# Three solve groups, GpSimd's share of the triangular solve, and scaling per group, in a ViT tower kernel

## What is computed

```python
k = x / norm(x); v = (x @ W_write.T) * beta; k_beta = k * beta        # beta = sigmoid(x @ W_beta.T)
A0 = tril(-(k_beta @ k.T * L), -1)                                    # L = decay ** (i - j)
A = solve_triangular(eye - A0, eye, lower=True, unit_diagonal=True)   # 37x37, one per image and head
v_new = A @ v
o = tril(k @ k.T * L) @ v_new
out = x + o @ W_read.T
```

## Time and profile before

| what | value |
|---|---|
| median of three runs | 836.0 us (835.88 to 836.0) |
| the profiled execution | 836.92 us, span of its instructions 835.1 us |
| mean granted TensorE clock | 0.886 of full speed |
| busy share of the span | TensorE 81%, VectorE 54%, ScalarE 27%, GpSimd 31% |

### The profile page before, as it was taken

The page is one execution under the profiler, slowest core; times in us unless marked ns, Lnnn a source line. Parts: engine busy times, 40 slices in busy tenths (PEclk is TensorE's granted clock), DMA queues, the critical chain, the costliest instruction groups (busy, mean ns, idle before and its releaser), DMA issues. The chain is left out here.

```text
span 835.1 us, 13690 instructions
## 1 busy us (share of the span) xinstructions
PE 678.3 (81%) x4562; PEld 519.5 (62%) x4562; DVE 448.1 (54%) x1266; ACT 229.1 (27%) x635; POOL 260.3 (31%) x418
## 2 busy tenths in 40 slices
PE   5899999999977149999983385196569999999994
PEld 4567677777755139999972364085436767667673
DVE  1567777777765742444799199466613333333321
ACT  0223333333322043443431022032013232232321
...
DMA packets 24643, 49.77 MB, mean 60 GB/s; under 512 B 15284, under 2 KB 15414, under 8 KB 23936
## 3 DMA queue, kind: packets, MB, share of 16 engines
...
q10 hardware_dynamic: 288, 4.25, 1.3%
...
## 5 line engine op out<-in xcount | busy, mean ns | idle before, releaser
L1762 PE MATMUL psum<-arena_w,work 128*128 x208 | 95.9, 605 | 1.0 <-DVE work L1814 1.0
L1860 ACT ACTIVATE work<-psum,cst 128x128 f32<-128x128 f32 x208 | 56.6, 383 | 144.1 <-PE psum L1775 144.1
L1786 PE MATMUL psum<-arena_w,work 128*128 x416 | 94.2, 379 | 0.4 <-ACT work L1860 0.4
L1786 PEld LDWEIGHTS psum<-arena_w,work 128*128 128x128 f32 x416 | 77.1, 190 | 10.5 <-issue 1.1
L1724 POOL DMA_INDIRECT out<-work,row_i x26 | 25.8, 990 | 160.2 <-DVE work L1836 160.2
L1823 DVE COPY work<-psum 128x512 f32<-128x512 f32 x52 | 36.0, 692 | 70.0 <-PE psum L1762 61.9
L346 PE MATMUL psum<-arena_w 128*111 128x256 f32 x264 | 64.1, 396 | 4.9 <-DMA arena_w<-in_pack 4.9
L1762 PEld LDWEIGHTS psum<-arena_w,work 128*128 128x128 f32 x208 | 38.3, 194 | 40.1 <-issue 40.1
L711 POOL TENSOR_TENSOR arena_w<-arena_w,work 101x592 f32<-101x592 f32 x33 | 39.6, 1200 | 72.2 <-DVE work L577 72.2
L346 PEld LDWEIGHTS psum<-arena_w 128*111 128x111 f32 x264 | 46.5, 183 | 19.7 <-issue 9.6
L1130 PE MATMUL psum<-tokens,work 111*111 111x128 f32 x88 | 18.2, 340 | 43.4 <-POOL work L1537 43.4
...
...
## 6 DMA issues: line engine op xcount, KB each, us to landing
arena_w<-in_w SPq DMA_DIRECT2D x2, 4096.0 KB, 13.3
...
work<-a_rows SPq DMA_DIRECT2D x21, 32.4 KB, 2.0
```

The lines of the kernel that those rows point to most:

```text
L1762: mm = nc.tensor.matmul(bank[2 * j + f][:, :], xgt[j][:, k * 128:(k + 1) * 128], arena_w1[:, bass.ds(expert * (2 * FF) + (k * FF + f * 512 ...
L1786: mm = nc.tensor.matmul(bank[7][:, 0:D], ht[j][:, g * 128:(g + 1) * 128], arena_w2[:, bass.ds(expert * (FC * D) + g * D, D)], start=(g == ...
L1860: nc.scalar.activation(ht[j][:, g * 128:(g + 1) * 128], bank[4 + f][:, k * 128:(k + 1) * 128], ACT.Gelu, bias=cst[:, bass.ds(expert * FC + ...
```

## The change

There are three groups, pairs 0 to 4, 5 to 7 and 8 to 10; the third has four sets of partitions. The rows stored for a system are now the folded attention products (so the system is held transposed, with its stored rows as columns), and a 38th column carries the strength. VectorE scales and negates the whole group once (`prepare`) and reads the system with a stride of 38 numbers. The first 16 columns of the inverse are VectorE's, by product and reduction; the other 21 are GpSimd's, by product and addition of one column at a time (`substitution` with `which`), in slots of its own program. A group counts as solved when both are done. Group 1 is held in `arena_w1`, group 2 in the first half of `arena_w2`. `normalise` and `normalise_outputs` move from VectorE to ScalarE, with a bias that GpSimd computes; the router's transposes and logits are four tiles back. GpSimd's order in a turn and SyncE's order of stores and loads change. The tables `lag` and `keep` and the product `ln` go. The core of the diff:

```diff
+NW = TOK + 1
 RL = 112
-GROUPS = ((0, 6), (6, PAIRS))
-SLOTS = (1.0, 1.0, 5.0, 1.7)
+GROUPS = ((0, 5), (5, 8), (8, PAIRS))
+SLOTS = (1.0, 7.0, 0.8, 3.5, 1.0)
...
             ec = carver(arena_w1, n1w + n2w)
-            lt, ln = ec(H1 * R, R), ec(H1 * R, R)
+            lt = ec(H1 * R, R)
...
+            def place_of(g):
+                if g == LAST:
+                    return arena_w2[:, 0:TOK * NW], arena_w2[:, TOK * NW:TOK * (NW + TOK)]
+                if g == 0:
+                    return sys_n, sys_x
+                return arena_w1[:, 0:TOK * NW], arena_w1[:, TOK * NW:TOK * (NW + TOK)]
+            def products_of(g):
+                space = arena_w2[:, TOK * (NW + TOK):] if g == LAST else work[:, NT * NE:]
+                return space[:, 0:16 * TOK], space[:, 16 * TOK:16 * TOK + 21 * 21]
+            def substitution(eng, ops, g, which):
+                im0, im1, nb, stride, sets = group_of(g)
+                used = (sets - 1) * stride + H1 * nb
+                cols = -(-TOK // sets)
+                split = 16 // sets
+                rows_n, rows_x = place_of(g)
+                x = rows_x[0:used, 0:cols * TOK].rearrange("p (c i) -> p c i", c=cols)
+                n = rows_n[0:used, :].rearrange("p (j i) -> p i j", j=TOK)
+                for i in range(which * split * sets, TOK - which):
+                    most = min(cols, i // sets + 1)
+                    c0, c1 = (split, most) if which else (0, min(split, most))
+                    if c0 >= c1 or i == which == 0:
+                        continue
+                    j0, j1 = (i + 1, TOK) if which else (0, i + 1)
+                    shape = [used, c1 - c0, j1 - j0]
+                    w = products_of(g)[which][0:used, 0:(c1 - c0) * (j1 - j0)].rearrange("p (c j) -> p c j", c=c1 - c0)
+                    free(eng, chain[which], steps[which])
+                    if which:
+                        ops.tensor_tensor(w, x[:, c0:c1, i:i + 1].broadcast_to(shape),
+                                          n[:, j0:j1, i].unsqueeze(1).broadcast_to(shape), ALU.mult).then_inc(chain[which], 1)
+                        eng.wait_ge(chain[which], steps[which] + 1)
+                        ops.tensor_tensor(x[:, c0:c1, j0:j1], x[:, c0:c1, j0:j1], w, ALU.add).then_inc(chain[which], 1)
+                    else:
+                        ops.tensor_tensor(w, x[:, c0:c1, j0:j1], n[:, i, j0:j1].unsqueeze(1).broadcast_to(shape),
+                                          ALU.mult).then_inc(chain[which], 1)
+                        eng.wait_ge(chain[which], steps[which] + 1)
+                        ops.tensor_reduce(x[:, c0:c1, i], w, AX_X, ALU.add).then_inc(chain[which], 1)
+                    steps[which] += 2
+                    yield (c1 - c0) * (j1 - j0)
+                eng.wait_ge(chain[which], steps[which])
+                ops.engine_nop().then_inc(solved[g], 1)
+            def advance(queue, budget, fixed, each):
+                while queue and budget > 0:
+                    size = next(queue[0], None)
+                    if size is None:
+                        queue.pop(0)
+                    else:
+                        budget -= fixed + each * size
+            steps = [0, 0]
+            begun = {}
+            ends = {GROUPS[g][1] - 1: g for g in range(len(GROUPS))}
+            firsts = {2 * GROUPS[g][0]: g for g in range(len(GROUPS))}
...
                 def load_systems(g):
+                    rows_n, _ = place_of(g)
-                    if g:
-                        sp.wait_ge(solved[g - 1], 1)
+                    if g == LAST:
+                        sp.wait_ge(z1_done, PAIRS)
                 def store_inverses(g):
-                    sp.wait_ge(solved[g], 1)
+                    _, rows_x = place_of(g)
+                    sp.wait_ge(solved[g], 2)
-                                src = sys_x[h * nb:(h + 1) * nb, :]
+                                src = rows_x[h * nb:(h + 1) * nb, :]
-                                src = sys_x[s * stride + h * nb:s * stride + (h + 1) * nb, 0:cols * TOK].rearrange(
+                                src = rows_x[s * stride + h * nb:s * stride + (h + 1) * nb, 0:cols * TOK].rearrange(
...
-                    if g:
-                        store_inverses(g - 1)
+                        if t == NT - NB and g == LAST > 0:
+                            store_inverses(0)
+                            load_inverses(0)
                     load_systems(g)
-                for g in range(LAST):
+                for g in range(1, LAST):
+                    store_inverses(g)
                     load_inverses(g)
                 sp.wait_ge(v_done, NT)
                 sp.wait_ge(g_done, NT)
...
-                for t in range(NT + 3):
+                for t in range(NT + 4):
-                    turn_outputs(t - 3)
+                    turn_outputs(t - 4)
-                    router_logits(t - 3)
+                    router_logits(t - 4)
...
+                def normalise(i):
+                    if not pair_of(i):
+                        return
+                    act.wait_ge(powered1, i + 1)
+                    free(act, turned1, i - 1)
+                    free(act, summed, i - 1)
+                    for j in range(2):
+                        last = nc.scalar.activation(xn[i % 2][:, j * D:(j + 1) * D], h_pair(i)[:, j, :], ACT.Identity,
+                                                    bias=st1[:, 16 + j:17 + j], scale=st1[:, 14 + j:15 + j])
+                    last.then_inc(normed1, 1)
+                def normalise_outputs(t):
+                    if not tile(t):
+                        return
+                    act.wait_ge(powered2, t + 1)
+                    nc.scalar.activation(x_half(t), h_rows(t), ACT.Identity, bias=ve2[t % 2][:, 2:3],
+                                         scale=ve2[t % 2][:, 1:2]).then_inc(normed2, 1)
...
+                    normalise(i - 1)
                     copy_gates(i + 1)
                     activate(i, range(HB // 2, HB))
                     squares(i - 1)
-                for t in range(NT + 3):
+                for t in range(NT + 4):
+                    normalise_outputs(t - 3)
                     copy_solved(t)
-                    copy_turned(t - 3)
+                    copy_turned(t - 4)
                     copy_attended(t)
             @block.vector
...
+                    nc.vector.tensor_tensor(attn_t[:, t * H1 * R:(t + 1) * H1 * R], bank[7][0:R, 0:H1 * R], lt,
+                                            ALU.mult).then_inc(n_masked, 1)
+                def prepare(g):
+                    rows_n, rows_x = place_of(g)
+                    if g == LAST:
+                        dve.wait_ge(z1_done, PAIRS)
+                    nc.vector.memset(rows_x[:, 0:cols * TOK], 0.0).then_inc(zeroed[g], 1)
                     for s in range(sets):
                         own = len(range(s, TOK, sets))
                         end = 128 if s == sets - 1 else (s + 1) * stride
+                        nc.vector.memset(rows_x[s * stride:end, s:s + (own - 1) * (TOK + sets) + 1:TOK + sets],
+                                         1.0).then_inc(zeroed[g], 1)
                     dve.wait_ge(n_in[g], 16 * H1 * sets)
+                    n = rows_n.rearrange("p (j i) -> p j i", j=TOK)
+                    nc.vector.scalar_tensor_tensor(n[:, :, 0:TOK], n[:, :, 0:TOK], -1.0,
+                                                   n[:, :, TOK].unsqueeze(1).broadcast_to([128, TOK, TOK]),
+                                                   ALU.mult, ALU.mult).then_inc(diagonal[g], 1)
+                    dve.wait_ge(diagonal[g], 1)
+                    nc.vector.memset(rows_n[:, 0:TOK * NW:NW + 1], 1.0).then_inc(diagonal[g], 1)
+                    dve.wait_ge(diagonal[g], 2)
+                queue = []
+                turn_no = [0]
+                def solve_some(budget):
+                    advance(queue, budget, 0.42, 0.0021)
+                def all_steps(g):
+                    begun[g] = turn_no[0]
+                    prepare(g)
+                    yield 700
+                    yield from substitution(dve, nc.vector, g, 0)
...
                 for i in range(-1, PAIRS + 2):
+                    turn_no[0] = i
                     gate_second(i - 1)
                     gate_first(i)
+                    solve_some(SLOTS[0])
                     decay_products(i - 2, 0)
                     add_outputs(i - 1)
                     decay_products(i - 2, 1)
+                    solve_some(SLOTS[1])
+                    if i - 2 in ends:
+                        queue.append(all_steps(ends[i - 2]))
+                for t in range(NT + 4):
+                    turn_no[0] = PAIRS + 2 + t
+                    while t in firsts and len(queue) > LAST - firsts[t]:
+                        solve_some(0.1)
                     add_read(t - 1)
+                    keep_logits(t - 4)
                     if t > 0:
+                        solve_some(SLOTS[2])
...
```

(39 more changed lines are left out.)

137 lines of the change are left out of this document (14 added, 123 removed).

## The result

The changed kernel is slower: 854.48 us, the median of 4 runs (851.65 to 856.88), against 836.0. The ratio is 1.022, with a 95% interval of 1.0182 to 1.0258. The profiled execution took 856.23 us with a span of 854.4, where before it was 835.1: 19.3 us more on the profile's clock. The forecast was 847.5. Sign and places were right, and 7 us are missing. The last fold comes 10.0 us later than forecast, the tile loop gives some of that back, and 2.3 us are added behind it.

A forecast was written before the change was run, and what follows sets the result against it. TensorE bounds turns without a solve, VectorE those with; then last fold, first spread, tiles, remaining solve and DRAM trip form one chain. Its end moves from 582.1 to 593.6, +11.5: span 846.6, median 847.5; forecast 839 to 853, range 833.5 to 858.

The forecast's parts named there:

- Rival C: Solve turns and first emptied queue: engines lock each other out, 0.34 for half of GpSimd's instructions; +8, 855; chance 0.13.
- rival B: VectorE's solve: strided reads of the system cost 0.7 ns more per element; +9.5, so 857; chance 0.12.
- The term of 0.65: Turns 2 to 6: strengths ahead of the power and ScalarE's normalising lengthen each turn by 0.65 us, 3.3 in all.
- VectorE as the bound: Turns with a solve: VectorE's work sets their length, 65.7 us for turns 7 to 11.
- The stride: VectorE's reads of the system at a stride of 152 bytes: taken to cost nothing extra.
- The scaling: Scaling and clearing ahead of each group's solve: some 2070 elements and five fixed parts, 2.9 us.
- my 0.35: Turns with a solve: VectorE's contention with GpSimd, 0.35 us per turn, near the low end of 0 to 3.4.
- The emptied queue: Ahead of tile 0: GpSimd does 21 queued steps, 15.3 us plus 1.0 contention; first spread at 478.1, was 472.8.
- Rival D: First spread: the DRAM trip and not GpSimd's queue decides, no net change; 836; chance 0.07.
- Both holes: Tile loop: GpSimd's 14 forced steps ahead of tile 10, 9.5 us; 14 steps left ahead of tile 16, 9.9 us.
- sign that I named for being wrong: Tile loop: wrong if the hole ahead of tile 10 is missing, or fewer than ten steps are left at tile 16.
- The trip over DRAM ahead of tile 16: Last group's inverses, stored and loaded back behind its solve: 9.2 us, so that spread comes at 564.9.

The follow-up runs named there:

- e1: Changed kernel with GpSimd's old order in a turn put back (power before second strengths, add before second fold): 850.68 us.
- e3: Changed kernel without the transposition, so VectorE reads the system's row as neighbouring elements (inverses then differ): 849.00 us.
- e5: Changed kernel with the edits of e1 and e2 together: 836.12 us, ratio 1.001 to the kernel before.
- e8: e5 with GpSimd's solve budget a turn at 5.0 in place of 3.5: 834.83 us.
- e4: Changed kernel with GpSimd's share of the solve left out (last 21 columns of each inverse incomplete): 826.74 us.
- e2: Changed kernel where GpSimd, ahead of a group's first tile, finishes only that group's solve steps, not its whole queue: 839.99 us.
- e6: e8 with groups due 3 tiles sooner, VectorE's budget a tile 1.2 in place of 0.8, and a solve slot at tile 0: 823.51 us.
- e10: e6 with solved signals right behind the last step, GpSimd's solve steps left out of turn 12 and cut to budget 2.0 in turn 11: 821.90 us.

## Why the prediction was right in sign and 7 us short

| step | forecast | measured |
|---|---|---|
| turn without a solve | 12.35 | 12.96 |
| turn 7 starts | 391.7 | 394.43 |
| turns 7 to 10 | 14.5, 12.4, 13.3, 13.2 | 16.09, 13.14, 14.59, 15.31 |
| turn 11 starts | 445.1 | 453.56 |
| last fold | 461.8 | 471.8 |
| last fold to first spread | 16.3 | 17.1 |
| first spread | 478.1 | 488.87 |
| first spread to that of tile 16 | 86.8 | 83.8 |
| spread of tile 16 to last add | 23.5 | 21.2 |
| last add to the end of the span | 258.2 | 260.5 |
| median | 847.5 | 854.48 |

In these rows the last fold is 10.0 late, the wait behind it 0.8 longer, the tile loop 5.3 shorter and the end 2.3 longer: 7.8 on the span, 7.0 on the median. So the total came out nearer than the last fold by luck: errors of opposite sign met. 854.48 lies 1.5 us above the band of 839 to 853 that I gave the forecast itself, close to what I had for rivals C (855) and B (857), of which C did not happen and B only in part.

- **The order of GpSimd.** The mechanism was right, and e1 shows it alone. The term of 0.65 was mis-sized: it measured 1.25. From the tanh to TensorE's turning of the rows I had 3.48 us and it is 4.05 (386.74 to 390.79). ScalarE's pair of normalisations takes 1.09 (0.99 until the next operation starts) and not the 0.75 that I took over from VectorE's pair; the power and the bias take 1.33 and not 1.15. Over five turns that is 3.0 us, of which 2.7 show at the start of turn 7, as turn 2 began 0.3 sooner than before.
- **The turns with a solve.** VectorE as the bound was right for turns 7 to 9; the four turns are 5.7 us longer than forecast. The counts of items (15, 11, 10 and 13) came out exactly; three prices were too small. The stride: I took nothing and kept 0.7 ns for rival B; e3 shows 0.7, its products in these turns are 3.4 us shorter in all (17.6 against 20.9), yet its turns only 1.4. The scaling: 2.60 us for 1369 elements where 0.153 + 0.00101n gives 1.54; with the clearing ahead of it, which was cheaper than I had it, the preparation takes 3.7 where I had 2.9, twice. GpSimd's long add: one product in each turn took 1.05 to 1.23 us in place of 0.2 to 0.6, 3.0 in all where my 0.35 in each of turns 8 to 10 make 1.1. These sum to 6.9, so 1.2 us elsewhere was priced too high; that wasn't told apart. Turn 11 is 12.3 in my sum where its own terms (3.2, 9.0 and 0.35) give 12.55.
- **What I put at nothing** is GpSimd beside the scaling. In turn 10 the bias operations take 2.89 us beside it, and TensorE comes late and at a lower granted clock. In the changed kernel this costs some 0.3 us at most: in e1 and e5 the bias is done before the scaling starts, and their turn 10 is 15.03 and 15.04 long, here 15.31. In e8 it costs 1.1.
- **Rival C**, by which GpSimd's solve steps and VectorE's lock each other out turn by turn, was the wrong mechanism. e4 shows turns 8 and 9 unchanged to 0.01 us without those steps. Where the engines do meet is at two long operations, GpSimd's add and VectorE's scaling. The rule of the Trainium skill (SBUF — State Buffer, "Who interferes with whom"), that a VectorE instruction with two SBUF inputs and a GpSimd one that reads SBUF exclude each other, agrees with the rows all the same: the product begun at 419.43 beside the add of 418.78 to 420.17 ends at 420.52 (419.43 and 1.09), 0.35 behind the add, where the next product of its kind takes 0.50, while the reduction at 419.06, with one input, takes its usual 0.34. The bias operations beside the scaling agree too: they end at 447.04, the scaling at 446.74.
- **Rival B** was a true mechanism and too small alone: e3 gives back 5.5 of the 9.5 us that I counted. The Trainium skill (SBUF — State Buffer, "Door 1: The DMA port swizzle") has the penalty for a new 16-byte line at each access without a size; here it is 0.21 us for 296 elements at a stride of 152 bytes.
- **The emptied queue** was right in place and size: 21 steps as counted, 17.1 us between last fold and first spread (16.3 forecast), the spread released by GpSimd's own step. e2 takes it away, and the DRAM trip is late next, at 481.91. Rival D, by which the DRAM trip decides, is thereby refuted.
- **The tile loop.** Both holes were there, ahead of tile 10 behind GpSimd's forced steps (14 steps as counted, 8.6 us where I had 9.5; TensorE idle 7.96; adds at 522.65 and 534.69, 12.04 apart), and ahead of tile 16 behind VectorE's (552.58 to 576.24), again 14 steps as counted. Neither sign that I named for being wrong came. The trip over DRAM ahead of tile 16 was the term too large: 6.8 us from the first store (565.84) to the spread, where I had 9.2. The stretch behind the first spread took 5.3 us less than forecast, which gave back about half of the 10.8 that the first spread was late. From the last add to the end of the span it is 260.5 us, where it was 258.2 and I had left it so. The rows tell where the 2.3 us lie: from the last add to the end of the last logits it is 6.7 us (593.91 to 600.63) where it was 5.2, from there to the last issue 3.1 where it was 1.5, and behind that issue 250.7 where it was 251.5.
- **What I didn't see** is that the phase's end hangs on SyncE's 44 stores behind the last inverses. In the changed kernel they run from 574.24 to 600.46, the last logits end at 600.63, and the next issue comes 3.3 us behind the last store. Before, the stores ended at 580.62 and the logits at 582.06, and the next issue came 3.0 us behind the one and 1.5 behind the other. So some 1.6 of the 2.3 us above are the stores'. In e2, e6 and e10, too, the last logits end ahead of the last store.
